# Context tiles stored sequence by sequence: four short runs per partition in place of one long run

## The reference

```python
def _L0_xattn_ref(k, v, q, Wk, Wv, bv, Wq, bq, Wo, bo):      # k = v = ctx_1024
    kp = jnp.einsum('bsd,ed->bse', k, Wk)
    vp = jnp.einsum('bsd,ed->bse', v, Wv) + bv
    qp = jnp.einsum('bsd,ed->bse', q, Wq) + bq
    scores = jnp.einsum('bqd,bkd->bqk', qp, kp) * scale
    probs = jax.nn.softmax(scores, axis=-1)
    ctx = jnp.einsum('bqk,bkd->bqd', probs, vp)
    return jnp.einsum('bqd,ed->bqe', ctx, Wo) + bo
...
x = x + _L0_xattn_ref(ctx_1024, ctx_1024, _layernorm(x, axis=-1), ...)   # one head
x = x + _L0_attn_ref(_layernorm(x, axis=-1), ...)                        # 16 heads, relative positions
x = x + _L0_ffn_ref(_layernorm(x, axis=-1), ...)                         # 8 experts, top 2
x = x + _L1_xattn_ref(_layernorm(x, axis=-1), ctx_1024, ...)             # 16 heads
x = x + _L1_attn_ref(_layernorm(x, axis=-1), ...)                        # causal
x = x + _L1_ffn_ref(_layernorm(x, axis=-1), ...)                         # 8 experts, top 2
```

## Time and profile before

| | |
|---|---|
| median of 3 runs | 1574.12 us (1567.26 to 1579.7) |
| profiled execution, its own time | 1572.63 us |
| its span, first to last instruction | 1570.8 us |
| PE busy | 1264.7 us, 81% of the span |
| DVE busy | 996.1 us |
| ACT busy | 841.9 us |
| POOL busy | 835.7 us |
| mean granted TensorE clock | 0.899 of full speed |
| moved by DMA | 122.01 MB, mean 78 GB/s |

### The profile page before, as it was taken

The page is one execution under the profiler, slowest core; times in us unless marked ns, Lnnn a source line. Parts: engine busy times, 40 slices in busy tenths (PEclk is TensorE's granted clock), DMA queues, the critical chain, the costliest instruction groups (busy, mean ns, idle before and its releaser), DMA issues. The chain is left out here.

```text
span 1570.8 us, 48801 instructions
## 1 busy us (share of the span) xinstructions
PE 1264.7 (81%) x15330; PEld 1097.8 (70%) x15331; DVE 996.1 (63%) x3247; ACT 841.9 (54%) x2658; POOL 835.7 (53%) x1700
## 2 busy tenths in 40 slices
PE   3877788989729996799999999999969878449991
PEld 2655777878629886577777777777758767349991
DVE  4655367877346664577777777777759888433334
ACT  1555256565314443577777777777737665224450
POOL 2555024666636564466666666666534566646661
PEclk9999578788559998899999999999979999569996
DMA  7998552121112121312111111111000000122215
GB/s 223 261 263 218 213 165 76 58 63 53 35 49 73 59 62 37 113 62 91 33 50 33 50 34 43 40 37 43 15 15 3 16 24 23 45 61 68 70 58 169
DMA packets 91997, 122.01 MB, mean 78 GB/s; under 512 B 12689, under 2 KB 67218, under 8 KB 91858
## 3 DMA queue, kind: packets, MB, share of 16 engines
q1 hardware_dynamic: 74194, 82.77, 17.8%
q0 software_dynamic: 12288, 34.82, 7.4%
q10 hardware_dynamic: 5376, 2.63, 0.6%
HBM read 89.68 MB, written 30.49 MB: 76 GB/s over the span
## 5 line engine op out<-in xcount | busy, mean ns | idle before, releaser
L1592 ACT ACTIVATE p_prob<-six,p_nm 128x257 f32<-128x257 f32 x512 | 236.4, 475 | 132.1 <-DVE p_nm L1634 122.2
L1634 DVE TENSOR_REDUCE p_nm<-six 128x2 f32<-128x514 f32 x256 | 164.8, 686 | 12.9 <-PE six L1495 12.8
L1842 PE MATMUL bank<-sb_w,m_experts_aT 128*128 x1152 | 156.6, 279 | 7.6 <-ACT m_experts_aT L1871 4.9
L1821 POOL DMA_INDIRECT expert_outputs<-m_experts_y,m_experts_dest x144 | 142.7, 991 | 25.9 <-POOL m_experts_tiny L1820 11.4
L1858 PE MATMUL six<-m_experts_xT,m_experts_w 128*128 128x128 f32 x1152 | 156.0, 279 | 0.0
L1516 PEld LDWEIGHTS six<-sb_const,p_prob 128*128 128x128 f32 x1024 | 109.5, 141 | 65.5 <-issue 59.1
L1516 PE MATMUL six<-sb_const,p_prob 128*128 128x128 f32 x1024 | 137.0, 277 | 19.3 <-issue 17.5
L1842 PEld LDWEIGHTS bank<-sb_w,m_experts_aT 128*128 128x128 f32 x1152 | 141.1, 193 | 13.0 <-issue 12.8
L776 POOL DMA_INDIRECT expert_inputs<-p_r_x,p_r_slot x128 | 126.0, 984 | 41.2 <-issue 34.5
L1375 POOL TENSOR_TENSOR p_score<-p_score,p_mx 128x512 f32<-128x512 f32 x64 | 67.2, 1049 | 147.8 <-DVE p_mx L1320 145.9
L1858 PEld LDWEIGHTS six<-m_experts_xT,m_experts_w 128*128 128x128 f32 x1152 | 143.3, 196 | 0.6 <-issue 0.2
(11 more groups left out here) (287 smaller groups left out, 3498.2 us busy)
## 6 DMA issues: line engine op xcount, KB each, us to landing
ctxN_ring<-ctxN POOLq DMA_DIRECT2D x32, 516.0 KB, 10.6
ctxT_ring<-ctxT SPq DMA_DIRECT2D x32, 514.0 KB, 12.4
p_ctxT<-ctxT SPq DMA_DIRECT2D x32, 514.0 KB, 3.6
m_experts_x<-expert_inputs SPq DMA_DIRECT2D x144, 64.5 KB
bd_scores<-p_rows SPq DMA_DIRECT2D x32, 256.0 KB, 2.8
p_bd<-bd_scores SPq DMA_DIRECT2D x32, 256.0 KB
sb_w<-w SPq DMA_DIRECT2D x32, 256.0 KB
p_y<-expert_outputs SPq DMA_DIRECT2D x32, 128.0 KB, 3.3
```

The source lines that it names most:

```text
L1592: last = nc.scalar.activation(prob[:, b, g, :], scores_ps[:, g, 0:CTX], ACT.Exp, bias=nm[:, b % 2, g:g + 1], accum_out=total[:, b % 2, g:g ...
L1634: nc.vector.tensor_reduce(nm[:, b % 2, g:g + 2], scores_ps[:, g:g + 2, 0:CTX], AX.X, ALU.max, negate=True).then_inc(s[most], 1)
L1821: nc.gpsimd.indirect_dma_start(m.ys_dram[:, :], bass.IndirectOffsetOnAxis(ap=dest[:, t.par:t.par + 1], axis=0), y[:, t.par, :], None).then ...
L1842: last = nc.tensor.matmul(ps[6 + t.two][:, 0:D], aT[:, t.two, f * P:(f + 1) * P], m.w2[:, DS(held[p] + f * D, D)], start=(f == 0), stop=(f ...
```

## The change

Both forms are laid out sequence by sequence. For `ctxN` a sequence's 86 x 3 tokens stand together in memory (132,096 bytes), so that a partition of a tile gets four runs of 1536 bytes, 132,096 bytes apart. For `ctxT` each sequence gets 272 columns in place of 257, of which the last 15 are padding that is not loaded, so that a partition gets four runs of 1028 bytes, 1088 bytes apart, and a feature's row of all sequences is 139,264 bytes long in place of 131,584. Where the data stand in SBUF is unchanged, and so are the number of loads, who issues them, when, and what waits for them.

```diff
 RING, EARLY = 4, 2
+COLUMN_RUN = 272
 
 
 def context_columns(m, n):
-    return m.ctxT_dram[:, n * B4 * CTX:(n + 1) * B4 * CTX].rearrange("d (b k) -> d b k", k=CTX)
+    return m.ctxT_dram[:, n * B4 * COLUMN_RUN:(n + 1) * B4 * COLUMN_RUN].rearrange(
+        "d (b k) -> d b k", k=COLUMN_RUN)[:, :, 0:CTX]
 
 
 def context_rows(m, n):
-    return m.ctxN_dram[n:n + 1].rearrange("a p (b c d) -> p (a b) c d", b=B4, c=3)
+    return m.ctxN_dram[n * B4:(n + 1) * B4].rearrange("b p (c d) -> p b c d", c=3)
...
-                    sp.dma_start(ctxT[:, t.par], m.ctxT_dram[:, t.cols(B4 * CTX)].rearrange(
-                        "d (b k) -> d b k", k=CTX)).then_inc(ctx_in[t.par], 16)
+                    sp.dma_start(ctxT[:, t.par], m.ctxT_dram[:, t.cols(B4 * COLUMN_RUN)].rearrange(
+                        "d (b k) -> d b k", k=COLUMN_RUN)[:, :, 0:CTX]).then_inc(ctx_in[t.par], 16)
...
-        "ctxT": ctx[:, order].transpose(2, 0, 1).reshape(D, SEQS * CTX),
-        "ctxN": padded.reshape(TILES, B4, KC, 3, D).transpose(0, 2, 1, 3, 4).reshape(TILES, KC, B4 * 3 * D),
+        "ctxT": np.pad(ctx[:, order].transpose(2, 0, 1), ((0, 0), (0, 0), (0, COLUMN_RUN - CTX))).reshape(D, -1),
+        "ctxN": padded.reshape(SEQS, KC, 3 * D),
```

## The result

The changed kernel takes 1674.49 us (median of four runs, 1672.66 to 1677.39) against 1573.45 us for the kernel before: the ratio is 1.0643, with a 95% interval of 1.0612 to 1.0673. The prediction was 1580 and its range ended at 1608. The change is slower by 6.4%, some 101 us.

The account below looks back on a forecast made before the run. The prediction took `cross_one_head` to be DMA-bound: 1572.63 us of the profiled execution plus 7.9 us for shorter runs gave 1580.5, stated as 1580, with a range of 1550 to 1608.

Parts of the forecast that it names:

- What bounds the kernel now: In `cross_one_head`, the DMA engines were taken as the bound, with some 1.8 us of each 3.91 us step owed to them.
- The cost of shorter runs: Context loads in `cross_one_head`: about 7 ns per added run, 0.28 us a tile over 28 refill loads, 7.9 us in all.
- 214 x 21 / 16: Per tile in `cross_one_head`: 214 old runs, 21 ns more each, shared by 16 engines, giving 0.28 us.
- rival 4: `ctxN` loads in `cross_one_head` land on two engines, 12.5 us each; up to +240 us, 1813; chance 0.04.
- with the four in flight on different pairs, 3.1 us a tile and no loss: Milder branch of the few-engines rival: four `ctxN` loads on different engine pairs, 3.1 us a tile, no loss; rival's chance 0.04.
- The issuing instructions: SP and POOL load issues: longer issues stay hidden, L612 under 2.0 us, adding nothing to the forecast.
- The ends taken by number of runs: L612's issue on POOL for 344 runs: 2.27 us if paid per run, 3.15 us by a slope of 10 ns a run.
- L387 ahead of the setup's factors: In the setup, two longer load issues on POOL add 3 to 5 us; part of the POOL-bound rival, chance 0.22.
- Relief: Runs of context loads in `cross_one_head` meet less, -19 us, giving 1554; chance 0.22.
- No change of pieces: Context loads: the pieces the engines see stay the same, as data are one run in SBUF; 1573; chance 0.04.
- The second pass that reads: `cross_many_heads`: 0.17 us more per `ctxT` load costs nothing, since SP waits 14.3 us before each.

Follow-up runs that it names:

- e9: The kernel before with `ctxN` on 128 partitions (chunks of 128, 128 and 1 tokens) and both its loads issued by SP instead of POOL; ratio 0.9838.
- e3: The changed kernel with each sequence's `ctxN` block padded to 96 rows, so a load brings 96 partitions; 1577.67 us, 1.003 of the kernel before.
- e1: The kernel before with only the new `ctxT` form, `ctxN` left as it was; ratio 1.0017.
- e8: The changed kernel with rings of six instead of four and POOL's `ctxN` load issued two steps earlier; ratio 1.054 to the kernel before.
- e12: The changed kernel with `ctxN` padded to 88 partitions instead of 86; ratio 1.0141 to the kernel before.
- e7: The kernel before with `ctxN` on 128 partitions (chunks of 128, 128 and 1 tokens), its two loads issued by POOL; ratio 0.9895.
- e4: The changed kernel with each `ctxN` load cut into four, one per sequence, with one run a partition; ratio 1.004 to the kernel before.

## Why the prediction was wrong

- **What bounds the kernel now**: right in kind. The pass was DMA-bound: in `e9`, with more rate for the loads, its last product starts 28 us earlier (127.3 against 155.4). The size was off: some 1.8 us of a step were put down to the DMA engines, from steps at the end in which L446, the scores, no longer runs. With PE busy all the time a step takes 2.87 us, which leaves 3.91 - 2.87 = 1.0 us.
- **The cost of shorter runs**, 7 ns a run, 7.9 us in all: the size holds within what can be told. `e3`, which has all the short runs and 12% more `ctxN` bytes, costs 0.3% (0.03 to 0.57), 0.5 to 9 us; `e1` 0.17%. My value of 1580 is close to `e3`'s ratio on this chip, 1.003 x 1573.45 = 1578, which is to say to a change that keeps the engines.
- **The step that failed** is the division by 16 engines in the cost of shorter runs, "214 x 21 / 16": the 344 runs of a `ctxN` load went to two engines (share 0.25 with two loads out) and the load landed after 19.4 us in place of 10.6, so that a step took 6.71 us where the sum has 0.28 more than before (3.68 by the same measure). The prediction had this as rival 4, "`ctxN` lands on few engines", and its chance of 0.04 was far too low: one run a partition was shown and four were not, which is an unknown and no reason for so small a chance. By the rule of the Trainium skill ("DMA: Bandwidth & Descriptors", section on why a DMA increments its semaphore by 16, on how many engines share a load), 86 gives 2. The runs agree, for GpSimd once a partition has several runs and for SP with one run, and 88 gives 11.
- And inside that rival, **"with the four in flight on different pairs, 3.1 us a tile and no loss"** was the branch that came true, with a wrong price. The pairs do differ, and 12.5 us is near what the engines need: its packets add up to 11.0 us an engine with `ctxN` alone (57 of 191 ns and one of 68) and to 13.8 us beside `ctxT` (57 of 241 and one of 77). But 12.5 / 4 assumes that four loads are always in flight and that nothing else is: with `ctxT`'s packets on the same engines a load lands after 19.4 us, and the buffer is filled again only 6.3 us after its load was used, since L612 stands behind the next step's work in POOL's order. (20.7 + 6.3) / 4 = 6.76 us, against 6.71 measured. Only `e8` had more loads out, and it gave back about 1%, so a share of the loss is loads that slow each other, and no run prices it.
- **The issuing instructions**: L612 came to 1.93 us, just under the 2.0 from which I had POOL decide. The ends taken by number of runs (2.27 and 3.15 us) were wrong in kind: 0.57, 0.72, 0.84 and 1.93 us were measured at 6, 24, 32 and 172 places an engine, though 384 runs were issued in 0.72 us and 344 in 1.93. It is not quite a straight line: 0.52 us + 8.2 ns a place gives 0.78 at 32, where `e12` had 0.84 and `e7` 0.82. POOL sets the pace inside a burst (3.9 us from 98.42 to 102.34) but not over a cycle.
- **L387 ahead of the setup's factors**, 3 to 5 us in that rival: the loss in front of the first step was 7.6 us, and it is the barrier that waits for the landing (38.51 - 30.92 = 7.6), which I had not seen in the trace of before although POOL stands idle there.
- **Relief**: nothing of it; `e3` and `e4` are slower than before by 0.3 and 0.4%. The argument that 86 partitions stay 86 partitions held, and `e7` showed that this was where the relief lay. The port rule of the Trainium skill ("SBUF — State Buffer", section on the DMA port swizzle) agrees in sign: with 128 partitions the load alone went from 229 to 342 GB/s, and the even split of `e3` did not do it. That the ports are the cause fits the estimate by halves but is not shown by itself.
- **No change of pieces**, rival 3: false. The packets of `ctxT` went from 4112 to 1028 bytes, though the data are one run on the SBUF side.
- **The second pass that reads**: right, 3.8 us to land and no loss.

## What to carry to other kernels

When the shape of a load changes, ask first over how many DMA engines it will be spread, and only then what its runs cost: here the engines were worth 6 to 17% of the kernel and the runs at most 0.6%. An outermost size that 16 divides kept all engines in every form tried (96 from GpSimd, 128 from either queue); 86 worked for one queue and one form only. A price such as "load time over loads in flight" holds only if the program's order keeps that many in flight, so count from the use that frees a buffer to the issue that fills it, and look at what the issue stands behind.

## What the runs showed of the hardware that was not expected

- A load issued by GpSimd over k engines still puts packets on the others: the counts fit as many places on each of the other 16 - k, filled with 4-byte pieces (798 packets of 12 bytes a load at k = 2, 50 at k = 11, none with 96 partitions), and the issue is paid by places an engine, some 8 ns each between 6 and 172.
- Successive GpSimd loads with k = 2 took different engines (four busy for two loads, share 0.25; up to eight data packets at once for four); successive SP loads of 86 partitions took the same two (each began when the one ahead was through, two data packets at a time, share 0.27 with `ctxT` beside them, 11.8 us a step).
- The barrier after the setup lets go only when loads issued by GpSimd have landed: 28.0 us with none out, 30.9 and 38.5 us with two out that land at 30.1 and at 37.6.
- POOL had five `ctxN` loads with k = 2 out and then stood, in both kernels with larger rings. With rings of eight, POOL issued five back to back from 48.01 us, and the next issue then stood 13.92 us; with rings of six the sixth stood until 0.3 us after a landing. The limit is not a number of loads, since `e4`, with 6 places an engine for each load, had up to nine out. A limit on open places (five loads have 860 an engine) would fit and was not tried.
